# Recommender attention kernel: masked and weighted sums each in one piece, query one tile late, ordered first loads, 17 row dots on VectorE

## The chip, the cores and the metric

The kernel runs on one core of one Trainium2 chip. The metric is the device time of one execution in microseconds (us). Engines are named as in the profile: PE is TensorE, DVE is VectorE, ACT is ScalarE, POOL is GpSimd, SP is SyncE.

## The reference

For each of 512 users there are 200 history items of 128 numbers, with a mask, an age and a popularity per item. All is float32 but the mask. Cut to what matters:

```python
decay = exp(-(softplus(decay_alpha) + 1e-6) * age) * mask
mean_hist = (items * mask[..., None]).sum(1) / (mask.sum(1) + 1e-6)
q = mean_hist @ Wq.T; k = items @ Wk.T; v = items @ Wv.T
scores = (q . k) * 128**-0.5 + log(decay + 1e-12)      # -inf where masked
long_term = softmax(scores) @ v
# short_term, mean_pop, mean_rec: means over the 5 items at positions cnt-5 .. cnt-1
g = sigmoid([mean_pop, mean_rec] @ gate_w.T + gate_b)
user = g * short_term + (1 - g) * long_term
out = layernorm(user) * ln_gamma + ln_beta
```

The kernel never forms k and v. It multiplies the mean with the product of Wq and Wk once (`wqk`), takes the dot of that query with each item row, and applies Wv to the weighted sum of rows.

## The kernel before, in words

**Tiles.** A tile is 16 users, 3,200 rows of items. It lies on 128 partitions: 8 partitions to a user and 25 rows of 128 numbers on each partition, 1.6 MB in one load. There are 32 tiles, in 16 pairs; 4 pairs (8 tiles, 128 users) make a group, and there are 4 groups. `x` has 8 slots in SBUF; the load of tile n waits until the weighted sums of tile n-8 are done (L235).

**One tile's way through the engines.** POOL spreads the mask into a block matrix (`build_mblk`, L277). PE multiplies it with the 25 rows, which gives the masked sums (50 matmul records, L368). ACT divides by the count (`copy_sums`, L480), PE folds that to a mean (`make_mean`, L375), ACT copies it (L491), PE turns it into the query (`make_query`, L382) and ACT copies the query to SBUF (`copy_query`, L498). Then the 25 row dots are shared out. DVE does 18 of them as one instruction with an accumulator read each (`dots`, L734), reading the query from PSUM. For the other 7, POOL multiplies (`products`, L297, in chunks of 4 and 3 rows) and ACT sums each row (`sum_products`, L471). DVE adds the logarithm of the decay and takes the maximum over each user's 8 partitions in five small steps for a pair of tiles (`user_maxima`, L681 to L707). ACT exponentiates (L506), POOL spreads the weights (`build_pblk`, L286), PE makes the weighted sums (L368), ACT copies them (L487) and PE folds them into the group's bank (`fold_rows`, L390).

**Groups.** Once a group's eight tiles are folded, DVE, PE and POOL finish it (Wv, the short-term sum, the norm) in between the dots of the next group. For this POOL gathers the last five items of each user once a group (`gather`, L330 and L333), and raises the variance to a power (L305).

**Order.** Each engine works through an order that is written out by hand, in steps of one pair. All waits are on semaphores, and an engine that waits does nothing that stands behind. On PE a step does the masked sums of one tile, then the weighted sums of an earlier tile, cut at `CUTS` into three pieces: the mean is put between the first and the second, the query between the second and the third. So the query of a tile is made in that tile's own half step. On ACT the copy of a query stands in front of the last sums of the tile before it. Weighted sums run five tiles behind masked sums (`WX_BEHIND`).

**Start.** SP issues the mask for all tiles in one load whose runs are 25 bytes (`mask_p`), three weight loads, the mask by user, the first tile, five small loads, the second tile, the ages, the third tile, and then waits for eight gathers of POOL before the fourth tile (L249). DVE waits for all five small loads (L599) before the start of the decay's scale. POOL issues those eight gathers (L355) in a row before its first products. DVE prepares the decay and the gate between the dots of the first tiles (L613 to L651), with short vectors held in SBUF.

Of the kernel before, what the change touches and what calls it, by code (L numbers as in the profile page):

```python
# [42 lines left out]
SLOTS = GP * PAIR  # L43
# [3 lines left out]
CUTS = ((7, 15), (3, 11))  # L47
SUM_COL, WX_COL = (0, 0), (1, 1)
MEAN_AT = 2 * D
WX_BEHIND = 5  # L50
LAST_PAIR = NPAIR - 1

KEPT_AT, FIRST_KEPT = 9, 4
# [6 lines left out]
DOTS = 18  # L60
GPROD = ROWS - DOTS
GCHUNKS = ((0, 4), (4, GPROD))
POOL_IDENT = 5
POOL_IOTA = 7
POOL_CONSTANTS = 15
DVE_BANKS = 3
# [4 lines left out]
def build(nc, items, mask, age, pop, Wq, Wk, Wv, gate_w, gate_b, gamma, beta, decay_alpha, out):  # L71
    items_t = items.rearrange("u t d -> (u t d)").rearrange("(g p n) -> g p n", p=P, n=ROWS * D)
    items_rows = items.rearrange("u t d -> (u t) d")
    mask_t = mask.rearrange("u t -> (u t)").rearrange("(g p r) -> p g r", p=P, r=ROWS)
    age_t = age.rearrange("u t -> (u t)").rearrange("(g p r) -> p g r", p=P, r=ROWS)
# [4 lines left out]
    with ctx:  # L80
# [20 lines left out]
        mask_p = sb("mask_p", [P, NTILE, ROWS], U8)  # L101
        mask_f = sb("mask_f", [P, NTILE, ROWS])
        mask_u = sb("mask_u", [P, NGROUP, NITEM], U8)
        age_p = sb("age_p", [P, NTILE * ROWS])
        decay = sb("decay", [P, NTILE * ROWS])
# [3 lines left out]
        valid = sb("valid", [P, NGROUP, LAST])  # L109
        pop_valid, age_valid = sb("pop_valid", [P, NGROUP, LAST]), sb("age_valid", [P, NGROUP, LAST])  # L110
        cnt_p = sb("cnt_p", [P, NTILE])
        st = sb("st", [P, 16, NGROUP])
        soft = sb("soft", [P, 8])
# [25 lines left out]
        wx = sb("wx", [P, PAIR, D])  # L139
# [15 lines left out]
        own_v, rden_v = ps_dve[:, at + 2 * D:at + 2 * D + TU], ps_dve[:, at + 2 * D + TU:at + 2 * D + TU + 1]  # L155
        c_query = tuple(b[:, 0:D] for b in ps_query)
# [3 lines left out]
        ld_weights, ld_mask_p = sem("ld_weights"), sem("ld_mask_p")  # L160
        ld_mask_u, ld_age_p, ld_small = sem("ld_mask_u"), sem("ld_age_p"), sem("ld_small")
        last_gathered = sem("last_gathered")
        pool_setup, dve_setup, act_setup = sem("pool_setup"), sem("dve_setup"), sem("act_setup")
        wqk_done, wqk_ready = sem("wqk_done"), sem("wqk_ready")
        sp_exp_in, sp_exp, sp_ln_in, sp_ln, alpha_ready, decay_exp = (
            sem("sp_exp_in"), sem("sp_exp"), sem("sp_ln_in"), sem("sp_ln"), sem("alpha_ready"), sem("decay_exp"))
        decay_floored, decay_ln = sem("decay_floored"), sem("decay_ln")
# [29 lines left out]

        def has(s, back, n=NPAIR):

            return 0 <= s - back < n  # L200
# [19 lines left out]
        def _(sp):  # L220
# [5 lines left out]
            def load(s, k, t):  # L226
                i = k * PAIR + t
                sp.dma_start(x[:, i, :], items_t[bass.ds(s * PAIR + t, 1), :, :].rearrange("g p n -> (g p) n")
                             ).then_inc(x_loaded[i], 16)

            def step(g, k):
                s = g * GP + k
                for t in range(PAIR):
                    if has(s, GP):
                        sp.wait_ge(wx_done, (s - GP) * PAIR + t + 1)  # L235
                    load(s, k, t)

            sp.dma_start(mask_p[:, :, :], mask_t).then_inc(ld_mask_p, 16)
            for dst, src in ((wq, Wq), (wk, Wk), (wv, Wv)):
                sp.dma_start(dst[:, :], src).then_inc(ld_weights, 16)  # L240
            sp.dma_start(mask_u[:, :, :], mask_n).then_inc(ld_mask_u, 16)
            load(0, 0, 0)
            sp.dma_start(gw[:, :], gate_w.broadcast_to([P, 2])).then_inc(ld_small, 16)
            for dst, src in ((da, decay_alpha), (gb, gate_b), (gam, gamma), (bet, beta)):
                sp.dma_start(dst[:, :], src.unsqueeze(0).broadcast_to([P, src.shape[0]])).then_inc(ld_small, 16)
            load(0, 0, 1)
            sp.dma_start(age_p[:, :].rearrange("p (g r) -> p g r", r=ROWS), age_t).then_inc(ld_age_p, 16)
            load(1, 1, 0)
            sp.wait_ge(last_gathered, 2 * NGROUP * 16)  # L249
            load(1, 1, 1)  # L250
            steps(step, NPAIR - 1, first=2)
# [6 lines left out]
        def _(pool):  # L258
# [12 lines left out]
            def build_mblk(s, k):  # L271

                for t in range(PAIR):
                    if has(s, 2):
                        pool.wait_ge(sum_done, (s - 2) * PAIR + t + 1)
                    m = mask_f[:, bass.ds(s * PAIR + t, 1), :].rearrange("p g r -> p (g r)")
# [60 lines left out]
            def step(g, k):  # L337
                s = g * GP + k
                if has(s, 1):
                    products(s - 1, k - 1, 1)  # L340
# [521 lines left out]
```

## Time and profile before

| what | us |
|---|---|
| median of 3 runs | 196.67 (195.12 to 198.18) |
| the profiled execution, its own time | 197.98 |
| its span, first to last instruction | 196.2 |
| DVE busy | 162.5 |
| PE busy | 154.2 |
| POOL busy | 142.8 |
| ACT busy | 110.2 |

The profiled execution is one run. Its span leaves out 1.8 us of its own time, and that time is 1.3 us above the median. Busy times are per engine and overlap each other.

### The profile page before, as it was taken

How to read it: one execution, taken by the hardware profiler on the slowest of the kernel's cores; microseconds unless marked ns; L12 is line 12 of the kernel's file. 1: busy time of each engine (PE TensorE's matmuls, PEld its weight loads, DVE VectorE, ACT ScalarE, POOL GpSimd, SP SyncE). 2: the span in 40 equal slices, each digit the busy share in tenths (PEclk: the TensorE clock that was granted, in tenths of full speed). 3: DMA queues.
4: the chain of work that ended last, by engine and by line, in shares of the span. 5: the costliest groups of instructions: out<-in, count | busy, mean ns of one | idle time of the engine just before them, and what ended most of it. 6: DMA issues, size and time to landing. Idle time of an engine off the chain costs nothing.

```text
span 196.2 us, 9396 instructions
## 1 busy us (share of the span) xinstructions
PE 154.2 (79%) x3413; PEld 122.0 (62%) x3413; DVE 162.5 (83%) x1345; ACT 110.2 (56%) x646; POOL 142.8 (73%) x167
## 2 busy tenths in 40 slices
PE   0254734886999797999999899898997977998890
PEld 0152523573787676787787677677785756777780
DVE  1521999999999999869999998969999876958943
ACT  2002074595587566477778667655777455478420
POOL 3367984587779896777998989786989687467411
PEclk9999988698799999699999999999999999699998
DMA  6949979999589999889899899999888999400000
GB/s 35 279 171 329 189 261 398 435 429 408 185 309 331 404 356 336 314 319 336 326 384 354 345 428 354 348 358 342 323 326 303 419 352 337 160 5 17 5 3 13
DMA packets 15710, 55.57 MB, mean 283 GB/s; under 512 B 10160, under 2 KB 11312, under 8 KB 11568
## 3 DMA queue, kind: packets, MB, share of 16 engines
q1 hardware_dynamic: 15088, 53.64, 76.0%
q0 software_dynamic: 576, 1.33, 2.0%
q8 instruction: 27, 0.44, 0.9%
q14 instruction: 19, 0.16, 0.2%
HBM read 54.70 MB, written 0.26 MB: 280 GB/s over the span
## 4 chain that ended last, share of the span: by engine, by line
POOL 29%; PE 28%; issue 17%; DMA 13%; ACT 6%; DVE 5%; POOLq 0%; DVEq 0%; ACTq 0%
PE ps_acc L368 22%; POOL gprod L297 14%; DMA x<-in_r_hist_items_dram 10%; POOL mblk L277 4%; POOL pblk L286 4%; ACT gprod L471 3%; PE ps_query L382 3%; DMA mask_p<-in_r_hist_mask_dram 3%; DVE junk_v L734 3%; POOL pop_taken L355 2%; POOL age_taken L355 2%; PE ps_acc L375 2%; PE ps_group L390 2%; ACT sums L480 1%; DVE decay L617 1%
## 5 line engine op out<-in xcount | busy, mean ns | idle before, releaser
L734 DVE SCALAR_TENSOR_TENSOR junk_v<-x,ps_query 128x128 f32<-128x128 f32 x576 | 127.9, 278 | 12.7 <-ACT query L498 12.6
L297 POOL TENSOR_TENSOR gprod<-x,query 128x512 f32<-128x512 f32 x64 | 72.2, 1150 | 21.6 <-ACT query L498 21.5
L368 PE MATMUL ps_acc<-x,mblk 128*16 128x128 f32 x1600 | 66.1, 300 | 11.0 <-DMA x<-in_r_hist_items_dram 7.9
L368 PE MATMUL ps_acc<-x,pblk 128*16 128x128 f32 x1600 | 70.7, 281 | 3.3 <-issue 1.8
L471 ACT ACTIVATE gprod<-gprod 128x128 f32<-128x128 f32 x224 | 66.1, 299 | 3.8 <-POOL gprod L297 3.7
L368 PEld LDWEIGHTS ps_acc<-x,mblk 128*16 128x16 f32 x1600 | 51.9, 105 | 18.5 <-DMA x<-in_r_hist_items_dram 9.8
L368 PEld LDWEIGHTS ps_acc<-x,pblk 128*16 128x16 f32 x1600 | 45.5, 98 | 10.3 <-issue 3.4
L734 DVE DVE_READ_ACCUMULATOR junk_v<-x,ps_query 128x1 f32 x576 | 46.6, 81 | 0.1
L471 ACT ACTIVATION_READ_ACCUMULATOR gprod<-gprod 128x1 f32 x224 | 42.8, 191 | 0.0
L480 ACT ACTIVATE sums<-ps_acc,rcnt_rows 128x128 f32<-128x128 f32 x32 | 11.7, 366 | 43.5 <-PE ps_acc L368 43.5
L286 POOL TENSOR_TENSOR pblk<-own,ex 128x400 f32<-128x400 f32 x32 | 27.2, 868 | 10.9 <-ACT ex L506 10.9
L277 POOL TENSOR_TENSOR mblk<-own,mask_f 128x400 f32<-128x400 f32 x32 | 27.1, 867 | 4.7 <-DVE mask_f L581 4.6
L382 PE MATMUL ps_query<-wqk,mean_p 128*128 128x128 f32 x64 | 16.7, 345 | 4.8 <-ACT mean_p L491 4.8
L375 PE MATMUL ps_acc<-fold,sums 128*128 128x16 f32 x64 | 12.9, 276 | 8.0 <-ACT sums L480 7.8
L375 PEld LDWEIGHTS ps_acc<-fold,sums 128*128 128x128 f32 x64 | 9.8, 193 | 13.7 <-ACT sums L480 13.7
L382 PEld LDWEIGHTS ps_query<-wqk,mean_p 128*128 128x128 f32 x64 | 10.2, 200 | 11.2 <-ACT mean_p L491 10.6
L487 ACT ACTIVATE wx<-ps_acc 128x128 f32<-128x128 f32 x32 | 8.5, 270 | 5.5 <-PE ps_acc L368 3.9
L506 ACT ACTIVATE ex<-kept,nmax_p 128x25 f32<-128x25 f32 x32 | 9.7, 307 | 2.8 <-DVE nmax_p L707 2.8
L390 PEld LDWEIGHTS ps_group<-fold,wx 128*128 128x128 f32 x64 | 8.5, 189 | 3.9 <-issue 3.4
L498 ACT ACTIVATE query<-ps_query 128x128 f32<-128x128 f32 x32 | 8.6, 270 | 4.1 <-PE ps_query L382 3.0
L390 PE MATMUL ps_group<-fold,wx 128*128 128x16 f32 x64 | 10.2, 268 | 0.3 <-ACT wx L487 0.3
L491 ACT ACTIVATE mean_p<-ps_acc 128x128 f32<-128x128 f32 x32 | 8.8, 273 | 1.5 <-PE ps_acc L375 1.4
(98 smaller groups left out, 90.8 us busy)
## 6 DMA issues: line engine op xcount, KB each, us to landing
x<-in_r_hist_items_dram SPq DMA_DIRECT2D x32, 1600.0 KB, 9.2
age_p<-in_r_hist_age_hours_dram SPq DMA_DIRECT2D x1, 400.0 KB, 14.5
out_dram<-y SPq DMA_DIRECT2D x4, 64.0 KB, 4.2
mask_p<-in_r_hist_mask_dram SPq DMA_DIRECT2D x1, 100.0 KB, 6.0
mask_u<-in_r_hist_mask_dram SPq DMA_DIRECT2D x1, 100.0 KB, 3.3
wq<-in_L_rec_Wq_dram SPq DMA_DIRECT2D x1, 64.0 KB, 5.6
wk<-in_L_rec_Wk_dram SPq DMA_DIRECT2D x1, 64.0 KB, 3.6
wv<-in_L_rec_Wv_dram SPq DMA_DIRECT2D x1, 64.0 KB, 3.5
```

The costliest lines, as they stand in the source:

```text
L277: nc.gpsimd.tensor_tensor(mblk[:, k % 2, t, :, :], own[:, :].unsqueeze(1).broadcast_to([P, ROWS, TU]), m.unsqueeze(2).broadcast_to([P, ROW ...
L286: nc.gpsimd.tensor_tensor(pblk[:, k % 2, t, :, :], own[:, :].unsqueeze(1).broadcast_to([P, ROWS, TU]), ex[:, t, :].unsqueeze(2).broadcast_ ...
L297: nc.gpsimd.tensor_tensor(gprod[:, t, a * D:b * D].rearrange("p (r d) -> p r d", d=D), rows((k % GP) * PAIR + t, r0 + a, r0 + b), query[:, ...
L368: ins = nc.tensor.matmul(dst[c:c + TU, 0:D], blk[:, k % 2, t, m, :], x[:, i + t, m * D:(m + 1) * D], start=(m < CG), stop=(m >= ROWS - CG))
L375: nc.tensor.matmul(mean_cols(s, t), sums[:, t, :], fold[:, :], start=True, stop=True).then_inc(mean_done, 1)
L382: nc.tensor.matmul(c_query[t], mean_p[:, t, :, :].rearrange("p u c -> p (u c)"), wqk[:, :], start=True, stop=True).then_inc(query_done, 1)
L390: ins = nc.tensor.matmul(ps_group[:, c + t * TU:c + (t + 1) * TU], src[:, t, :], fold[:, :], start=True, stop=True)
L471: ins = nc.scalar.activation(src, src, ACT.Copy, accum_out=score[:, k % 2, t, DOTS + r:DOTS + r + 1])
L480: nc.scalar.activation(sums[:, t, :], sum_bank(s, t)[:, 0:D], ACT.Copy, scale=rcnt_rows[:, bass.ds(s * PAIR + t, 1)]).then_inc(sum_copied, 1)
L491: nc.scalar.activation(mean_p[:, t, :, :], mean_cols(s, t).unsqueeze(2).broadcast_to([P, TU, PU]), ACT.Copy).then_inc(mean_copied, 1)
L506: nc.scalar.activation(ex[:, t, :], kept[:, t, 0:ROWS], ACT.Exp, bias=nmax_p[:, t:t + 1], accum_out=wsum[:, i:i + 1]).then_inc(exp_done, 1)
L734: ins = V.scalar_tensor_tensor(out=junk_v[:, t, r, :], in0=x[:, (k % GP) * PAIR + t, r * D:(r + 1) * D], scalar=1.0, in1=c_query[t], op0=A ...
```

## The change

- **PE and ACT order.** The order is by slots of one tile. In slot n PE does the masked sums of tile n in one piece, the weighted sums of tile n-6 in one piece, the query of tile n-1, the mean of tile n, and after every second tile a fold at one place. `WX_BEHIND` is 6. Tiles 0 to 5 keep mean and query in their own slot. On ACT the copy of the query of tile n-1 stands behind all row sums of tile n-2 in the slots after the lead.
- **Buffers.** `x` has 10 slots; the weighted copy `wx` has two.
- **Row dots.** `DOTS` is 17. POOL multiplies and ACT sums 8 rows, in chunks of 4 and 4.
- **First transfers.** Mask and ages come as four blocks each of 32 partitions with long runs, and are brought to their tile layout by a transpose on DVE. Two mask blocks and the scalar `decay_alpha` are issued by ACT. SP issues tile 0 as its third load, and no longer waits for POOL's gathers. POOL issues two of the eight small gathers before its first products and the others in slots 1, 3 and 5.
- **Setup on DVE.** Most short vectors of the gate are in PSUM; the small constant is ACT's bias and not a DVE pass; the order of the pieces is changed; `wv` is turned later.

The core of the diff:

```diff
-SLOTS = GP * PAIR
+SLOTS = 10
-WX_BEHIND = 5
+WX_BEHIND = 6
-KEPT_AT, FIRST_KEPT = 9, 4
+KEPT_AT, FIRST_KEPT = 6, 4
-DOTS = 18
+DOTS = 17
@@ sync
+            def load(n):
+                i = n % SLOTS
+                if n >= SLOTS:
+                    sp.wait_ge(wx_done, n - SLOTS + 1)
+                sp.dma_start(x[:, i, :], items_t[n, :, :]).then_inc(x_loaded[i], 16)
+            for j in range(BLOCKS // 2):
+                sp.dma_start(mask_s[j * Q32:(j + 1) * Q32, :], mask_t[j, :, :]).then_inc(ld_mask_s, 16)
+            load(0)
+            for dst, src in ((wq, Wq), (wk, Wk)):
                 sp.dma_start(dst[:, :], src).then_inc(ld_weights, 16)
             sp.dma_start(mask_u[:, :, :], mask_n).then_inc(ld_mask_u, 16)
+            load(1)
+            for j in range(BLOCKS):
+                sp.dma_start(decay_s[j * Q32:(j + 1) * Q32, :], age_t[j, :, :]).then_inc(ld_age_s, 16)
+            load(2)
...
+            for n in range(4, NTILE):
+                load(n)
@@ gpsimd
+            def slot(n):
+                g, i = divmod(n, SLOTS_OF_GROUP)
+                if tile(n - WX_BEHIND + 1):
+                    build_pblk(n - WX_BEHIND + 1)
+                if i == 0 and has(g, 2, NGROUP):
+                    inverse_deviation(g - 2)
+                if tile(n + 2):
+                    build_mblk(n + 2)
+                if tile(n) and query_slot(n) == n:
+                    products(n)
+                if tile(n - 1) and query_slot(n - 1) == n:
+                    products(n - 1)
+                if i == 4 and g < NGROUP:
                     gather(g)
+                if n in (1, 3, 5):
+                    gather_context((n + 1) // 2)
@@ tensor
+            def slot(n):
+                g, i = divmod(n, SLOTS_OF_GROUP)
+                w = n - WX_BEHIND
+                if tile(n):
+                    masked_sums(n)
+                if n == 0:
+                    pe.wait_ge(ld_weights, 32)
+                    nc.tensor.matmul(ps_group[:, 0:D], wq[:, :], wk[:, :], start=True, stop=True).then_inc(wqk_done, 1)
...
+                if tile(w):
+                    weighted_sums(w)
+                if tile(n - 1) and query_slot(n - 1) == n:
+                    make_query(*divmod(n - 1, PAIR))
+                if tile(n):
+                    make_mean(*divmod(n, PAIR))
+                if tile(n) and query_slot(n) == n:
+                    make_query(*divmod(n, PAIR))
+                if tile(w - 1) and w % PAIR == 0:
+                    fold_pair(w // PAIR - 1)
@@ scalar
+            def slot(n):
+                w = n - WX_BEHIND
+                if n < WX_BEHIND:
+                    lead_slot(n)
+                else:
+                    if tile(n - 1) and query_slot(n - 1) == n:
+                        copy_mean(n - 1)
+                    if tile(n - 2) and query_slot(n - 2) == n - 1:
+                        sum_products(n - 2, 0, 2)
...
+                    if tile(n):
+                        copy_sums(n)
+                    if n > WX_BEHIND and tile(n - 2):
+                        sum_products(n - 2, 2, GPROD)
+                    if tile(n - 1) and query_slot(n - 1) == n:
+                        copy_query(n - 1)
...
+                if n % PAIR == 0 and n >= 2 * PAIR and n < NTILE + 1:
+                    exponential(n - 2 * PAIR)
+                    exponential(n - 2 * PAIR + 1)
...
+                if tile(w):
+                    copy_weighted(w)
@@ vector
+            def setup_mask():
+                dve.wait_ge(ld_mask_s, 16 * BLOCKS)
+                link(V.tensor_copy(hide_s[:, :], mask_s[:, :]))
+                V.transpose(mask_f[:, :, :].rearrange("p g r -> p r g"),
+                            hide_s[:, :].rearrange("p (q r) -> p r q", r=ROWS)).then_inc(mask_ready, 1)
...
+            setup_mask()
+            setup_counts()
+            setup_alpha()
+            setup_inverse_counts()
+            setup_hidden()
+            setup_wqk()
+            setup_first_rows()
             step(0, 0)
+            setup_valid()
+            steps(step, NPAIR + 3, first=1)
```

## Rows read from the trace of the kernel before

**Rows 1.** The page: busy time by engine, and two lines in 40 slices.
```profile
PE 154.2 (79%) x3413; PEld 122.0 (62%) x3413; DVE 162.5 (83%) x1345; ACT 110.2 (56%) x646; POOL 142.8 (73%) x167
...
DMA  6949979999589999889899899999888999400000
GB/s 35 279 171 329 189 261 398 435 429 408 185 309 331 404 356 336 314 319 336 326 384 354 345 428 354 348 358 342 323 326 303 419 352 337 160 5 17 5 3 13
```

**Rows 2.** Windows: busy us of PE, PEld, DVE, ACT, POOL; clock, DMA share, GB/s.
```profile
50.00:170.00 120.00, 108.49 (x2574) 86.81 (x2564) 110.40 (x983) 79.66 (x481) 98.44 (x106) 0.97 0.91 341
```

**Rows 3.** The page's groups of instructions: busy, mean ns of one, idle before.
```profile
L734 DVE SCALAR_TENSOR_TENSOR junk_v<-x,ps_query 128x128 f32<-128x128 f32 x576 | 127.9, 278 | 12.7 <-ACT query L498 12.6
L471 ACT ACTIVATE gprod<-gprod 128x128 f32<-128x128 f32 x224 | 66.1, 299 | 3.8 <-POOL gprod L297 3.7
```

**Rows 4.** Timeline of DVE, start and duration in us: dot, mask step, dot.
```profile
106.33 0.28 DVE L734 SCALAR_TENSOR_TENSOR junk_v<-x,ps_query 128x128 f32<-128x128 f32 x1
...
106.54 0.20 DVE L681 TENSOR_TENSOR kept<-score,ps_dve 128x50 f32<-128x50 f32 x1
106.66 0.28 DVE L734 SCALAR_TENSOR_TENSOR junk_v<-x,ps_query 128x128 f32<-128x128 f32 x1
```

**Rows 5.** Timeline of POOL from the seventh tile's products to the last tile's.
```profile
55.69 2.23 POOL L297 TENSOR_TENSOR gprod<-x,query 128x512 f32<-128x512 f32 x2
...
62.70 1.68 POOL L286 TENSOR_TENSOR pblk<-own,ex 128x400 f32<-128x400 f32 x2
64.35 2.24 POOL L297 TENSOR_TENSOR gprod<-x,query 128x512 f32<-128x512 f32 x2
...
67.54 1.02 POOL L333 DMA_INDIRECT taken<-in_r_hist_items_dram,group_row  x1 [0.82 <-POOL group_row L330]
...
178.77 2.25 POOL L297 TENSOR_TENSOR gprod<-x,query 128x512 f32<-128x512 f32 x2 [0.91 <-ACT query L498]
```

**Rows 6.** The chain that ended last, start and length: the first product chunk alone.
```profile
23.49 1.22 POOL gprod L297
```

**Rows 7.** Timeline of the start: mask, counts, first sums, scale, first dot.
```profile
6.88 0.58 DVE L581 CAST mask_f<-mask_p 128x800 f32<-128x800 uint8 x1 [4.78 <-DMA mask_p<-in_r_hist_mask_dram]
7.37 0.98 DVE L582 TENSOR_REDUCE cnt_p<-mask_p 128x32 f32<-128x800 uint8 x1
...
12.46 3.15 PE L368 MATMUL ps_acc<-x,mblk 128*16 128x128 f32 x50 [0.71 <-DVE cnt_rows L594]
...
14.59 0.95 POOL L355 DMA_INDIRECT pop_taken<-n_r_hist_popularity_dram,first_row  x1 [0.30 <-issue]
...
16.88 0.35 ACT L480 ACTIVATE sums<-ps_acc,rcnt_rows 128x128 f32<-128x128 f32 x1
...
19.39 0.29 DVE L734 SCALAR_TENSOR_TENSOR junk_v<-x,ps_query 128x128 f32<-128x128 f32 x1 [2.04 <-ACT query L498]
```

**Rows 8.** Timeline of DVE's setup: the hidden rows, and three gate steps.
```profile
23.15 2.94 DVE L613 TENSOR_SCALAR hide<-mask_f 128x800 f32<-128x800 f32 x1
...
34.41 0.16 DVE L636 TENSOR_TENSOR st<-st 128x4 f32<-128x4 f32 x1
...
49.26 1.04 DVE L648 TENSOR_TENSOR st<-st 128x4 f32<-128x4 f32 x1
```

**Rows 9.** DMA issues: size, median us from issue to landing; then the loads' spread.
```profile
mask_p<-in_r_hist_mask_dram SPq DMA_DIRECT2D x1, 100.0 KB, 6.0
mask_u<-in_r_hist_mask_dram SPq DMA_DIRECT2D x1, 100.0 KB, 3.3
...
DMA to landing us min/median/max: 6.7/9.2/21.6
```

**Rows 10.** Who waited for whom: total us, times, longest.
```profile
ACT ex L506 <- DVE nmax_p L707: 2.8, 2, 1.9
```

**Rows 11.** Timeline of the drain: PE's last weighted sums.
```profile
188.71 1.70 PE L368 MATMUL ps_acc<-x,pblk 128*16 128x128 f32 x50
```

More of the change, by code:

```diff
@@ L196, in steps, with slots, tile, query_slot @@
                 step(s // GP, s % GP)
+        def slots(slot, first=0):
+            for n in range(first, NTILE + WX_BEHIND + 3):
+                slot(n)
+        def tile(n):
+            return 0 <= n < NTILE
+        def query_slot(n):
+            return n if n < WX_BEHIND else n + 1
+        def at(s, t):
+            return (s * PAIR + t) % SLOTS
         def has(s, back, n=NPAIR):
@@ L316, in _ @@
                                 allow_small_or_imprecise_dtypes=True))
-            link(nc.gpsimd.tensor_copy(own_rows[:, :, :], own[:, :].unsqueeze(1).broadcast_to([P, CG * 2, TU])))
-            pool.wait_ge(mask_ready, 1)
-            build_mblk(0, 0)
+            assert made[0] == POOL_IOTA
             link(nc.gpsimd.memset(fold[:, :], 0.0))
@@ L357, in _ @@
                         in_offset=bass.IndirectOffsetOnAxis(ap=first_row[:, q:q + 1], axis=0)).then_inc(last_gathered, 16)
-            steps(step, NPAIR + 3)
+            pool.wait_ge(rows_ready, 1)
+            gather_context(0)
+            slots(slot)
             assert made[0] == POOL_CONSTANTS
@@ L379, in make_query @@
                 pe.wait_ge(mean_copied, s * PAIR + t + 1)
+                if not has(s, 1):
+                    pe.wait_ge(wqk_ready, 1)
                 if has(s, 1):
@@ L453, in _ @@
             pe.wait_ge(pool_setup, POOL_CONSTANTS)
-            pe.wait_ge(wqk_ready, 2)
             pe.wait_ge(cnt_ready, 1)
@@ L458, in _, with sum_products @@
             pe.wait_ge(dve_setup, DVE_BANKS)
-            steps(step, NPAIR + 3)
+            slots(slot)
         @block.scalar
         def _(act):
-            def sum_products(s, k, t, a, b):
+            def sum_products(n, a, b):
+                s, t = divmod(n, PAIR)
                 if a == 0 and has(s, 2):
@@ L551, in _ @@
             act.wait_ge(rcnt_rows_ready, 1)
-            step(0, 0)
-            act.wait_ge(alpha_ready, 1)
-            act.wait_ge(ld_age_p, 16)
-            nc.scalar.activation(decay[:, :], age_p[:, :], ACT.Exp, scale=soft[:, 5:6]).then_inc(decay_exp, 1)
-            act.wait_ge(decay_floored, 1)
-            nc.scalar.activation(decay[:, :], decay[:, :], ACT.Ln).then_inc(decay_ln, 1)
-            step(0, 1)
-            act.wait_ge(gate_in, 1)
-            nc.scalar.activation(st[:, 12:14, :], st[:, 10:12, :], ACT.Exp).then_inc(gate_exp, 1)
-            steps(step, NPAIR + 2, first=2)
+            slots(slot)
         @block.vector
```

395 lines of the change are left out of this document (184 added, 211 removed).

## The prediction, made before the changed kernel was run

> **What bounds the kernel now.** The page first: DVE is busy 83% of the span and POOL 73% [rows 1]. A share is only an average, so the windows come next. From 50 to 170 us DVE is busy 110.4 of 120 us, PE 108.5, POOL 98.4 and ACT 79.7, at a DMA share of 0.91 and 341 GB/s [rows 2]. Four resources lie within a quarter of each other. The groups name DVE's load, the 576 row dots, and what they wait for when they wait: ACT's copy of the query, 12.6 us in all, nearly all at the start [rows 3, 7].
>
> The timeline gives true prices, for DVE instructions overlap: a dot every 0.21 us (the mean of one is 278 ns), and 0.12 us for a maximum step between two dots [rows 4]. With five such steps a pair, a tile costs DVE 18 x 0.21 + 0.3 = 4.08 us. A group's finish and short-term sum are some 15 more instructions; at about 0.25 us each, between the two prices and the 0.35 us of longer ones (an estimate), that is 3.7 us a group.
>
> The steady stretch runs from the products of tile 6 at 55.69 to those of tile 31 at 178.77 [rows 5]: 123.1 us for 25 tiles, 4.92 each. DVE's sum for it is 25 x 4.08 = 102, three finishes 11.1, and about 4 for the last gate pieces: 117. So DVE alone explains all but 5%. POOL's sum before: products 2.24, two block builds 1.65 (from 62.70 to 64.35), so 3.89 a tile [rows 5]. The first 55.7 us are poor: the first dot starts at 19.39 [rows 7], and data comes at 35 to 329 GB/s in the first six slices, though 435 is reached in the eighth [rows 1].
>
> **The change part by part.**
>
> *First transfers.* Before, the mask's cast starts at 6.88 after a landing of 6.0 us [rows 7, 9]. Four blocks with long runs are issued from about 0.8 to 1.3 on two queues. The same bytes in longer runs land in 3.3 us (the mask by user) [rows 9]. I take 3.5 us, since the blocks are first in line: landed at 4.8; the other end is 6.0 us, landed at 7.3. Cast 0.58, then a transpose of 25 blocks of 32 columns, which no row shows: at the pace of the count over the same 800 elements it is 0.98 [rows 7]; the end above is the 2.94 of the slow pass over 800 elements [rows 8]. I take 1.1, nearest to the count. Mask ready at 6.6, counts at 7.7, PE's count sum and its copy to 8.4. Tile 0 is issued third, at about 1.7; the quickest load took 6.7 us [rows 9], so it also lands at 8.4. The first masked sums take 3.15 [rows 7], to 11.6. From ACT's first copy (16.88) to the first dot (19.39) it is 2.5 us [rows 7]; the weights' product now stands between, with 0.4 uncovered. First dot: 11.6 + 0.1 + 2.5 + 0.4 = 14.6, 4.8 us earlier. The decay's scale no longer waits for the other small loads. The other DVE setup ahead of the first dot (counts, scale, inverse, hidden rows, first rows) ends near 14.5 too: hidden by PE's masked sums, and if the hidden rows take 2.94 again, still inside them.
>
> On the two queues for the mask, the trace has no row. The Trainium skill (DMA: Bandwidth & Descriptors, "Issuing engines are not separate DMA queues") says that transfers issued from different engines share the same 16 DMA engines and that only issue time is saved. By that the second queue is worth about two issues, under 1 us; the sum above takes the gain from the run length and would stay.
>
> *Lead.* POOL starts when the first rows are known, about 14.7. The eight small gathers stood in one row ahead of its products at 1.25 us each (0.95 and the 0.30 before it) [rows 7]; now two do, six lie in slots 1, 3 and 5. Nothing of them is saved, they are only moved. Until the products of tile 6: two gathers 2.5, one block 0.8, then six products, ten blocks 8.3, six gathers 7.5, one group gather 2.0. Products with two chunks of four: a chunk of four is 1.22 [rows 6], so the chunk of three is about 1.0, and eight rows cost 2.49; six are 14.9. Sum 36.0: tile 6's products start at 50.7, against 55.69, 5 us earlier. DVE would be there near 45 (six tiles at 3.87, setup 7), so in the lead POOL is now last and the dot taken from DVE brings nothing there. Short vectors in PSUM help the gate: the same four-column product took 0.16 in one place and 1.04 in another, beside busy POOL [rows 8], and four such steps were slow. That is about 3 us, on DVE, which is no longer last here: costed at nothing.
>
> *Steady stretch.* DVE: 17 x 0.21 + 0.3 = 3.87 a tile; 25 tiles 96.8, finishes 11.1, rest 1: 109. POOL: 2.49 + 1.65 = 4.14 a tile, 103.5; three group gathers at 1.84 (1.02 and the 0.82 before it) [rows 5] and a small copy each, 6.1; three powers, no dearer than a block build, at most 2. POOL's sum is 111.6 and **POOL becomes the most loaded engine**. ACT: eight rows at 0.30 [rows 3] and six copies and exponentials of about 0.25, under 4 us a tile. PE loses a piece boundary and a wait on ACT's copy; since it is busy 108 of 120 with those waits in it, this gives slack and no time of its own. I keep the 5% that the stretch showed above its largest sum: 117.2 us instead of 123.1.
>
> *Loads.* Ten slots at six tiles' lag put one more load in flight, and SP is past all waits until tile 10. The rate needed is 52.4 MB over the 150 us to the last masked sums, 350 GB/s; reached were 435 in a slice [rows 1] and 341 at share 0.91 [rows 2], 375 at full share. Taken as covered by work; if the cover goes, each tile costs 1.64 MB at 341 GB/s, 4.8 us, which is where the kernel is now.
>
> Here a rule speaks against the change. The trace's best slice is 435 GB/s [rows 1]. The Trainium skill (SBUF — State Buffer, "A bandwidth-pool intuition that's wrong") gives about 358 GB/s between HBM and a core and calls HBM nearly always the end-to-end bottleneck; slices above it disagree. By it 52.4 MB take 146 us (an estimate from that page), the last tile lands near 150 us, and rival A below could hardly go under its 177; the forecast would stay.
>
> *Tail.* Before, from the last products to the end 17.4 us. Now: 2.49, four last row sums 1.2, five maximum steps without dots between 1.2, exponential 0.3, block 0.9, five hand-overs 0.8, then 7.5 as from PE's last weighted sums at 188.71 to the end at 196.2 [rows 11]: 14.4. The ends are 13.6 and the 17.4 of now.
>
> **Sum.** Span 50.7 + 117.2 + 14.4 = 182.3, from 196.2. The profiled execution's own time lies 1.8 above its span: 184.1. It stood 1.3 above the median of the runs, so against that median I say **183 us**.
>
> **The rivals.**
>
> *A. The engines mesh.* Deeper buffers take the 5% away: 50.7 + 111.6 + 14.4, 177 us. For it: part of the 5% was PE waiting for tiles that now come earlier. Against: DVE, POOL and ACT come within 3 to 12 us of each other over 25 tiles.
>
> *B. Lockstep.* The copy of a query stands behind all eight sums of the tile before, where it stood ahead of the last chunk's. So products, last four sums, copy, products form a loop of 2.49 + 1.2 + 0.3 + hand-overs, 4.2 us, just POOL's own 4.14; each gather or group finish then stops the others as well. With 12% instead of 5% over the sum: 125 us, 191 us in all. For it: four sums nearly equal. Against: POOL has two blocks to build while ACT sums.
>
> *C. Slower: the exponential blocks ACT.* In even slots ACT meets two exponentials before the next tile's copies. They need the maxima, whose last step comes 14 dots into a tile, 14 x 0.21 + 0.6 = 3.5 us, while ACT can be there 1 us into it. If DVE is the late one, ACT stands up to 2.5 us a pair with the next query behind it. It decides from 1.4 us a pair uncovered: 12.5 pairs, 17.5 us, over 200.6; all of it gives 214. Against: this wait cost only 2.8 us in two places before [rows 10], and the maxima now start three dots earlier.
>
> *D. The dot moved is no gain at all.* POOL's row costs 0.25 x 32 = 8 us while DVE's 6.7 is hidden: that is already in the sum, since POOL leads it.
>
> **How the numbers follow.** Forecast 0.48 (178 to 188), A 0.22 (172 to 178), B 0.22 (187 to 196), C 0.06, other 0.02. What a measurement can tell from no change is about 2%: 192.7 to 200.6. Faster: the forecast, A and seven tenths of B, 0.86; same: the rest of B, 0.07; slower: C and other, 0.07. The range reaches down to 173.5, which takes in the tail's and the mask's lower ends, and up to 192.5, which takes in B to its middle and the upper ends of mask and transpose (4 us).
>
> **What would show it.** First dot near 14.6 and tile 6's products near 51: start right. A steady stretch with POOL at 95% or more busy and DVE under it: forecast. Both under 90% with waits on the query's copy: B. Long waits of the exponential on the maxima: C. PE waiting long for tiles at a DMA share of 1: the loads. If the stretch per tile stays at 4.9 us, the prediction's main step is wrong.

## The result, and the profile after

| what | before | after |
|---|---|---|
| median of 20 runs each, us | 197.39 (193.71 to 201.57) | 201.62 (197.05 to 205.08) |
| ratio after to before | | 1.0147, 95% interval 1.0084 to 1.021 |
| the profiled execution, its own time | 197.98 | 204.02 |
| its span | 196.2 | 202.3 |

The changed kernel is slower by 1.5%, and certainly not faster; the forecast was 183 us and its range ended at 192.5. The profiled execution of it is one of its longer runs; five of the 20 took 197 to 200, so a few us of what follows belong to that run alone.

The page of after, busy times, the two lines in 40 slices and the queue by which PE gets its instructions (packets, MB, share of 16 engines), to be set beside [rows 1]:

```profile
PE 152.1 (75%) x3413; PEld 127.7 (63%) x3413; DVE 153.1 (76%) x1285; ACT 120.6 (60%) x710; POOL 151.9 (75%) x167
...
DMA  5999989999789899889999999998798802000000
GB/s 142 300 347 353 363 348 428 417 416 404 303 273 337 318 375 354 323 327 326 342 360 372 369 340 344 385 327 304 276 334 314 342 16 68 2 3 18 0 3 13
...
q8 instruction: 27, 0.44, 0.9%
```

No engine is above 76%. DVE has lost 9.4 us of work and POOL has gained 9.1, as the change says, and the span has grown. Two windows of after, columns as in [rows 2]: the one of [rows 2], and the steady stretch alone.

```profile
50.00:170.00 120.00, 99.53 (x2504) 86.85 (x2498) 98.65 (x882) 84.24 (x513) 102.47 (x103) 0.96 0.85 315
```

```profile
60.00:165.00 105.00, 87.67 (x2216) 76.37 (x2212) 92.12 (x830) 75.83 (x462) 90.49 (x91) 0.97 0.88 329
```

All four are idle 12% or more of the steady stretch, PE too, at 83% busy. So the answer lies in what they wait for. The groups, as in [rows 3]:

```profile
L811 DVE SCALAR_TENSOR_TENSOR junk_v<-x,ps_query 128x128 f32<-128x128 f32 x544 | 122.4, 280 | 21.2 <-ACT query L537 21.1
L314 POOL TENSOR_TENSOR gprod<-x,query 128x512 f32<-128x512 f32 x64 | 80.4, 1277 | 20.4 <-ACT query L537 20.2
L502 ACT ACTIVATE gprod<-gprod 128x128 f32<-128x128 f32 x256 | 75.8, 298 | 26.8 <-POOL gprod L314 25.3
```

DVE and POOL wait for ACT's copy of the query, and ACT waits for POOL's products: a ring. Before, the same two groups had 12.7 us (DVE) and 3.8 (ACT) of idle time [rows 3]. And of who waited for whom (total us, times, longest), one line of PE, which was 4.3 us in 7 times before:

```profile
PE ps_acc L392 <- issue: 12.9, 10, 2.4
```

The three stretches in which the prediction was summed:

| stretch | before | forecast | after | against forecast |
|---|---|---|---|---|
| start to the products of tile 6 | 55.69 | 50.7 | 56.97 | +6.3 |
| products of tile 6 to those of tile 31 | 123.1 (4.92 a tile) | 117.2 | 125.0 (5.00) | +7.8 |
| from there to the end | 17.4 | 14.4 | 20.3 | +5.9 |

**Start.** The timeline of after's start, as [rows 7]:

```profile
3.60 0.58 DVE L638 CAST hide_s<-mask_s 128x800 f32<-128x800 uint8 x1 [1.39 <-DMA mask_s<-in_r_hist_mask_dram]
4.22 1.70 DVE L639 STREAM_TRANSPOSE mask_f<-hide_s 128x800 f32<-128x800 f32 x1
...
9.74 3.14 PE L392 MATMUL ps_acc<-x,mblk 128*16 128x128 f32 x50 [2.05 <-issue]
...
15.64 0.28 DVE L811 SCALAR_TENSOR_TENSOR junk_v<-x,ps_query 128x128 f32<-128x128 f32 x1
```

The first dot is 3.75 us earlier than at 19.39 [rows 7], of 4.8 forecast. The rest is tile 0. It was issued at 1.70 and took 8.0 us to land, where 6.7 was counted, so it was there at 9.65, and PE starts at 9.74. The profile marks PE's 2.05 us of idle time "issue", but they are this wait; every run of the new order below has it, 2.05 to 2.69 us long. The DMA view of 0 to 3 us:

```profile
x<-in_r_hist_items_dram SPq DMA_DIRECT2D x1, 1600.0 KB, 8.0
```

**Lead.** The gain is gone by tile 6. ACT, POOL and DVE between 46 and 57 us:

```profile
51.96 0.32 ACT L548 ACTIVATE ex<-kept,nmax_p 128x25 f32<-128x25 f32 x1 [5.31 <-POOL pblk L302]
```

```profile
50.03 0.95 POOL L376 DMA_INDIRECT age_taken<-in_r_hist_age_hours_dram,first_row  x1 [0.30 <-issue]
...
56.97 2.51 POOL L314 TENSOR_TENSOR gprod<-x,query 128x512 f32<-128x512 f32 x2 [2.64 <-ACT query L537]
```

```profile
55.89 0.17 DVE L709 TENSOR_TENSOR pop_valid<-pop_taken,ps_fin 128x20 f32<-128x20 f32 x1 [7.59 <-DMA age_taken<-in_r_hist_age_hours_dram,first_row]
```

From the products of tile 5 (46.05) to those of tile 6 are 10.9 us, where 4.14 and two gathers (2.5) were counted. POOL does products, the last two small gathers (48.74 to 50.98) and then a block build. ACT's exponential waits 5.31 us for that build, and behind it on ACT stands the mean of tile 6; PE's next sums wait for the mean, the query comes behind them, and POOL then waits 2.64 us for the query. DVE stands 7.59 us for the last gather, to start the gate. The chain that ended last does not run through this wait, so whether it cost anything isn't shown.

**Steady.** Of the 25 spacings, 16 are 4.63 to 4.69 us; POOL shows why:

```profile
106.15 2.52 POOL L314 TENSOR_TENSOR gprod<-x,query 128x512 f32<-128x512 f32 x2 [0.48 <-ACT query L537]
108.61 0.87 POOL L302 TENSOR_TENSOR pblk<-own,ex 128x400 f32<-128x400 f32 x1
109.44 0.87 POOL L292 TENSOR_TENSOR mblk<-own,mask_f 128x400 f32<-128x400 f32 x1
110.80 2.52 POOL L314 TENSOR_TENSOR gprod<-x,query 128x512 f32<-128x512 f32 x2 [0.48 <-ACT query L537]
```

POOL's own work takes 4.17 and 0.48 is a wait each time. On ACT, from the end of those products (113.32) on:

```profile
113.35 0.31 ACT L502 ACTIVATE gprod<-gprod 128x128 f32<-128x128 f32 x1 [0.24 <-POOL gprod L314]
...
114.83 0.29 ACT L502 ACTIVATE gprod<-gprod 128x128 f32<-128x128 f32 x1
115.12 0.25 ACT L537 ACTIVATE query<-ps_query 128x128 f32<-128x128 f32 x1
```

Six sums, one each 0.295 us, and then the copy: 2.51 (products) + 1.77 + 0.25 + hand-overs 0.12 = 4.65. The call `sum_products(n - 2, 2, GPROD)` waits for the whole of the products, both chunks, before its first row; so six rows stand behind the second chunk and not the chunk's own four.

The other nine spacings are longer, 4.74 to 6.40: three have a group's gather (6.19 to 6.28), and four of the other six follow times in which **PE stands still with nothing to wait for** (the 6.40 follows the 2.42 us below). PE in the stretch between two of them, and the matmul behind the second (columns of windows; then the timeline, its idle time in brackets):

```profile
82.59:88.71 6.12, 5.90 (x126) 0.72 0.80 289
88.71:94.93 6.22, 4.67 (x126) 1.00 0.95 341
94.93:115.73 20.80, 19.50 (x505) 1.00 0.95 363
115.73:121.93 6.20, 5.39 (x126) 1.00 0.94 343
...
142.98:153.87 10.89, 9.26 (x252) 1.00 0.85 314
```

```profile
143.00 1.16 PE L392 MATMUL ps_acc<-x,mblk 128*16 128x128 f32 x33 [2.42 <-issue]
```

Between two pauses lie 126, 252 or 505 matmuls, multiples of 126 to within one, and each has its weight load: 252 instructions. The program has 3413 + 3413 of them, and 27 packets on the instruction queue: 253 to a packet. So PE pauses when it comes to the end of a block of instructions and the next is not there.

The trace also has the times of these packets; narrow windows of the DMA view place them. The window of 140.5 to 141.5 us holds the one that belongs to the pause above, from 140.58 to 141.47:

```profile
q8 instruction: 1, 0.02, 5.5%
```

Each of after's nine pauses in its sums (the wait for tile 0 is not one of them) ends 1.3 to 1.5 us after such a packet. In the fifteen traces of this document, 97 of the 99 pauses after 60 us end 1.2 to 1.7 us after one. Late is the packet's start and not its length: counted from PE's first matmul of the block before, the packet starts after 3.7 us in the median in after and 3.3 in before, but after 0.7 and 0.5 in e11 and e12 below, whose loads are light; it takes about 1 us in all four. Whether PE asks late or the request waits is not shown.

**Tail.** PE waits 2.92 us for the block of weights, which now stands behind the products of tile 31 on POOL, and then 100 matmuls take 5.29 us, 3.23 before. The window gives a granted clock of 0.60 of the upper level of 2.4 GHz, so most of it ran at 1.2:

```profile
185.34 2.46 PE L392 MATMUL ps_acc<-x,pblk 128*16 128x128 f32 x50 [2.92 <-POOL pblk L302]
188.70 5.29 PE L392 MATMUL ps_acc<-x,pblk 128*16 128x128 f32 x100
```

```profile
188.60:194.00 5.40, 5.40 (x102) 0.60 0.00 0
```

### The profile page after: what moved, and what is told of

It is laid out like the page before. It is cut to its first block, busy times and chain, and to the rows that moved or that the text cites. A ratio compares the mean times of both kernels' runs of the same rounds, so it can differ in the third digit from the quotient of the medians.

```text
span 202.3 us, 9424 instructions
## 1 busy us (share of the span) xinstructions
PE 152.1 (75%) x3413; PEld 127.7 (63%) x3413; DVE 153.1 (76%) x1285; ACT 120.6 (60%) x710; POOL 151.9 (75%) x167
## 4 chain that ended last, share of the span: by engine, by line
POOL 44%; issue 25%; DMA 12%; PE 8%; SPq 5%; ACT 4%; POOLq 1%; DVE 0%; ACTq 0%
POOL gprod L314 22%; DMA x<-in_r_hist_items_dram 12%; POOL pblk L302 10%; POOL mblk L292 8%; PE ps_acc L392 7%; ACT gprod L502 2%; POOL taken L352 2%; SPq L259 1%; SPq L249 1%; PE ps_query L408 1%; POOL rstd L322 1%; ACT ex L548 1%; SPq L265 1%; ACT query L537 1%; POOL pop_taken L376 0%
## 5 line engine op out<-in xcount | busy, mean ns | idle before, releaser
L811 DVE SCALAR_TENSOR_TENSOR junk_v<-x,ps_query 128x128 f32<-128x128 f32 x544 | 122.4, 280 | 21.2 <-ACT query L537 21.1
L314 POOL TENSOR_TENSOR gprod<-x,query 128x512 f32<-128x512 f32 x64 | 80.4, 1277 | 20.4 <-ACT query L537 20.2
L502 ACT ACTIVATE gprod<-gprod 128x128 f32<-128x128 f32 x256 | 75.8, 298 | 26.8 <-POOL gprod L314 25.3
L392 PE MATMUL ps_acc<-x,pblk 128*16 128x128 f32 x1600 | 60.6, 291 | 18.8 <-ACT mean_p L528 10.0
L392 PE MATMUL ps_acc<-x,mblk 128*16 128x128 f32 x1600 | 64.8, 303 | 11.4 <-issue 7.8
L392 PEld LDWEIGHTS ps_acc<-x,pblk 128*16 128x16 f32 x1600 | 49.8, 102 | 25.5 <-issue 16.4
L392 PEld LDWEIGHTS ps_acc<-x,mblk 128*16 128x16 f32 x1600 | 50.0, 106 | 18.0 <-issue 9.6
L502 ACT ACTIVATION_READ_ACCUMULATOR gprod<-gprod 128x1 f32 x256 | 48.3, 189 | 0.0
L811 DVE DVE_READ_ACCUMULATOR junk_v<-x,ps_query 128x1 f32 x544 | 44.9, 83 | 0.0
L513 ACT ACTIVATE sums<-ps_acc,rcnt_rows 128x128 f32<-128x128 f32 x32 | 11.4, 355 | 14.9 <-PE ps_acc L392 14.8
L408 PE MATMUL ps_query<-wqk,mean_p 128*128 128x128 f32 x64 | 17.1, 352 | 2.7 <-ACT mean_p L528 2.6
L376 POOL DMA_INDIRECT pop_taken<-n_r_hist_popularity_dram,first_row x4 | 4.1, 1037 | 8.7 <-DVE first_row L665 8.3
L322 POOL TENSOR_TENSOR rstd<-vare,half 128x1 f32<-128x1 f32 x4 | 2.3, 569 | 10.0 <-DVE vare L849 10.0
```

The costliest lines, as they stand in the source:

```text
L314: nc.gpsimd.tensor_tensor(gprod[:, t, a * D:b * D].rearrange("p (r d) -> p r d", d=D), rows(at(s, t), r0 + a, r0 + b), query[:, s % 2, t, ...
L392: ins = nc.tensor.matmul(dst[c:c + TU, 0:D], blk[:, s % 2, t, m, :], x[:, at(s, t), m * D:(m + 1) * D], start=(m < CG), stop=(m >= ROWS - CG))
L408: nc.tensor.matmul(c_query[t], mean_p[:, t, :, :].rearrange("p u c -> p (u c)"), wqk[:, :], start=True, stop=True).then_inc(query_done, 1)
L502: ins = nc.scalar.activation(src, src, ACT.Copy, accum_out=score[:, s % 2, t, DOTS + r:DOTS + r + 1])
L513: nc.scalar.activation(sums[:, t, :], sum_bank(s, t)[:, 0:D], ACT.Copy, scale=rcnt_rows[:, bass.ds(s * PAIR + t, 1)]).then_inc(sum_copied, 1)
L811: ins = V.scalar_tensor_tensor(out=junk_v[:, t, r, :], in0=x[:, at(s, t), r * D:(r + 1) * D], scalar=1.0, in1=c_query[t], op0=ALU.mult, op ...
```

## Experiments

Every run was made beside runs of the kernel before on the same chip ("before beside it"). For each profiled execution the table gives the start of tile 6's products, the mean per tile from there to tile 31, and PE's pauses of the line "issue" inside its sums, total and number, without the wait for tile 0. For after and before: 5.00 with 10.9 (9), and 4.92 with 4.3 (7).

| run | median us | before beside it | ratio, 95% | tile 6 | per tile | pauses |
|---|---|---|---|---|---|---|
| e1_split_sums | 199.43 | 199.04 | none | 58.55 | 4.97 | 12.8 (10) |
| e2_18_dots_new_order | 196.13 | 199.04 | 0.9834 (0.9767 to 0.9902) | 56.28 | 4.84 | 13.4 (11) |
| e3_17_dots_old_order | 199.56 | 199.04 | 0.9999 (0.9911 to 1.0087) | 55.30 | 5.04 | 3.1 (3) |
| e5_8_slots | 228.64 | 199.04 | none | 57.22 | 6.05 | 0.5 (1) |
| e6_two_in_flight | 196.08 | 199.31 | none | 56.86 | 4.87 | 12.4 (13) |
| e7_gathers_early | 194.58 | 199.31 | none | 53.31 | 4.78 | 15.6 (14) |
| e8_old_no_gather_wait | 202.40 | 199.31 | 1.0196 (1.0046 to 1.0346) | 57.87 | 5.00 | 7.7 (5) |
| e10_18_dots_split | 197.89 | 199.31 | 0.9912 (0.9724 to 1.0100) | 56.25 | 4.82 | 11.4 (11) |
| e11_new_light_loads | 197.67 | 198.76 | none | 58.18 | 4.84 | 1.0 (4) |
| e12_old_light_loads | 188.87 | 198.76 | 0.9534 (0.9385 to 0.9684) | 55.81 | 4.48 | 0 |
| e13_loads_in_pieces | 193.67 | 198.76 | none | 52.61 | 4.82 | 17.1 (15) |
| f2_18_early_light | 183.58 | 198.51 | 0.9428 (0.9261 to 0.9594) | 52.13 | 4.47 | 1.4 (2) |
| f1_18_early_again | 193.12 | 198.51 | 0.9878 (0.9692 to 1.0065) | 53.82 | 4.83 | 13.8 (10) |

Where the ratio is "none", only medians stand side by side.

### The ring on ACT: e1_split_sums

```diff
-                        sum_products(n - 2, 2, GPROD)
+                        sum_products(n - 2, 2, GCHUNKS[0][1])
+                        sum_products(n - 2, GCHUNKS[0][1], GPROD)
```

> The changed kernel, with the last six row sums of ACT split in two waits: rows 2 and 3 wait for POOL's first chunk alone, rows 4 to 7 for the second. Nothing else differs. Loop theory (the query's copy stands behind six sums that all wait for POOL's second chunk, which sets 4.65 us between two tiles' products): the spacing falls by the two sums, 0.59 us, to about 4.17 (POOL's own sum 4.16), and the time by 22 x 0.48 = 10 us less what other waits take back: 191 to 195 us. Rival, pauses and loads (PE's pauses and late tiles set the pace): spacing stays at 4.6 or more, time within 2 us of the changed kernel's 201.6.

POOL of e1, the products of two tiles in a row, now without a wait for the query:

```profile
105.25 2.51 POOL L314 TENSOR_TENSOR gprod<-x,query 128x512 f32<-128x512 f32 x2
...
109.54 2.53 POOL L314 TENSOR_TENSOR gprod<-x,query 128x512 f32<-128x512 f32 x2
```

The usual spacing fell from 4.65 to 4.30 (4.17 was expected), so the ring is real and was rightly named. The time did not follow: 199.43 us, where 191 to 195 was expected. The mean per tile moved only from 5.00 to 4.97, and PE's pauses rose from 10.9 to 12.8 us. So in the full run the ring is not the only thing that holds the pace.

### The moved dot: e2_18_dots_new_order and e3_17_dots_old_order

e2 is after with `DOTS = 18`; e3 is before with

```diff
-KEPT_AT, FIRST_KEPT = 9, 4
+KEPT_AT, FIRST_KEPT = 8, 4
-DOTS = 18
+DOTS = 17
```

> The changed kernel with 18 row dots on DVE and 7 on POOL and ACT (chunks 4 and 3). Loop theory: the loop is shorter by one product of POOL (0.27) and one sum of ACT (0.29): 4.65 becomes 4.09, and DVE's own 4.08 a tile plus the groups' finish becomes the largest sum, so 25 tiles take 5 to 9 us less than in the changed kernel: 193 to 197 us. Rival, 17 dots are the gain and other parts the loss: DVE, now at 4.5 us a tile with the finish, makes it 3 to 6 us slower than 201.6.

> The kernel before with 17 row dots on DVE and 8 on POOL and ACT, the maxima one dot earlier so that the last step still fits; the old order stays. If DVE bounded the kernel before as the prediction says, its 6.7 us less show at least in part: 191 to 195 us. If POOL's extra 0.27 us and ACT's 0.29 us a tile lie in the loop in the old order too, no gain or a loss: 196 to 202 us.

POOL of e2:

```profile
99.69 2.25 POOL L314 TENSOR_TENSOR gprod<-x,query 128x512 f32<-128x512 f32 x2
...
103.78 2.25 POOL L314 TENSOR_TENSOR gprod<-x,query 128x512 f32<-128x512 f32 x2 [0.20 <-ACT query L537]
```

With the dot back on DVE the new order is 5.5 us under after's 201.62 and 1.7% faster than before, with an interval clear of 1. The usual spacing is 4.09: the ring is shorter by 0.26 (products) and 0.3 (one sum). In the old order the same dot costs and gains nothing that can be measured. A likely reason is that there the copy of the query stands in front of the last sums; no run tried this alone. So the two parts of the change do not fit each other. And taking 6.7 us of dots from DVE gained nothing in the old order either, so DVE's work alone was not what held that kernel back in the full run.

### Both: e10_18_dots_split

> The changed kernel with 18 dots and ACT's last sums in two waits (rows 2 and 3 for the first chunk, rows 4 to 6 for the second). The loop of 4.09 us loses its two sums and falls to POOL's own 3.9; DVE's own sum (4.08 a tile and 3.7 a group) and the pauses of PE then set the pace. Loop theory: least spacing 3.9, gain over 18 dots alone at most 2 us, 194 to 196. Rival (DVE is the bound and its maxima are in the way): no gain, 196 to 198.

e2 and e1 together. The usual spacing is 4.02 (3.9 was expected) and the mean 4.82, both hardly under e2's 4.09 and 4.84; the median, 197.89, is above e2's. At 18 dots the ring is POOL's own length and splitting has little left to give.

### The gathers of slot 5: e7_gathers_early

```diff
-                if n in (1, 3, 5):
-                    gather_context((n + 1) // 2)
+                if n in (1, 2, 3):
+                    gather_context(n)
```

> The changed kernel with 18 dots, the small gathers in slots 1, 2 and 3 in place of 1, 3 and 5. Lead theory (the 10 us between the products of tiles 5 and 6 come from the gathers of slot 5: DVE waits for the last of them, ACT's exponential for POOL's block behind them): products of tile 6 start at 51 to 54 us and not at 56.3, and the time falls by 2 to 5 us, to 191 to 194. Rival (PE at its lower clock sets the lead): products of tile 6 stay within 1 us of 56.3, time as with 18 dots alone, 196.

On top of e2. Tile 6's products start at 53.31 instead of 56.28, 3.0 us earlier, and the profiled span is 3.2 us less than e2's. f1_18_early_again is the same kernel with more runs:

> The changed kernel with 18 dots and gathers in slots 1, 2, 3 once more, in five rounds, for an interval against the kernel before: if the row of dots given to POOL and the gather of slot 5 were the losses, it stands at 0.965 to 0.985 of before; if the 194.6 of its first run was luck, at 0.99 to 1.00.

It has the lowest median of the kernels that compute the whole, 193.12 against 198.51 beside it, but its interval just takes in 1, and 0.9878 is just above the 0.965 to 0.985 expected.

### What PE's pauses hang on

**Buffers.** e5 is after with `SLOTS = 8`.

> The changed kernel with 8 slots for tiles in place of 10, so that at most one or two loads stand in the queue while PE works. Theory on PE's pauses (12 us of pauses inside runs of matmuls, all before the last load lands, come from queued loads ahead of the instruction fetch): fewer loads in flight give shorter pauses, under 8 us, but late tiles come instead. Rival (the pauses have nothing to do with the depth of the load queue): pauses as before at 10 to 13 us, and late tiles make it slower by 3 to 10 us.

```profile
PE ps_acc L392 <- DMA x<-in_r_hist_items_dram: 38.6, 19, 3.8
...
PE ps_acc L392 <- issue: 3.0, 2, 2.6
```

The ten slots are needed: at six tiles' lag eight make PE wait 38.6 us for tiles. Of the 3.0 us marked "issue", 2.59 are the wait for tile 0, so one pause of 0.45 is left. Two things changed at once: PE is slower, so its instructions have more time to come, and the DMA share from 60 to 165 us is 0.75 and not 0.88. The run does not tell them apart.

**Depth of the load queue.** e6 is e2 with SP waiting for tile n-2 before it issues tile n; **size of its pieces**: e13 is e7 with each tile in five loads of five rows.

> The changed kernel with 18 dots (196.1 us, 18 us of PE pauses), and SP issues tile n, from 4 on, only when tile n-2 has landed: at most two loads in flight, ten slots as before. Queue theory (PE's pauses inside runs of matmuls come from its instruction fetch standing behind queued loads): the pauses fall from 18 us to under 8, the tiles still come in time, 25 tiles take 5 to 8 us less, 189 to 192 us. Rival (the pauses come from PE using up its instructions in bursts, whatever is queued): pauses stay at 14 to 20 us, time within 2 us of 196, or above if tiles come late.

> The changed kernel with 18 dots and gathers in slots 1, 2, 3 (194.6 us), and each tile loaded by five transfers of 5 rows (2,560 bytes a partition) and not by one of 25 rows (12,800 bytes). If a fetch of instructions waits for the transfer that an engine is in, shorter ones let it in sooner: pauses fall from 18.7 us to under 9, time 188 to 192 us. Rival (the fetch waits for its share of full engines, whatever the piece): pauses 14 us or more, time 193 to 197.

Neither lowers the pauses much: 12.4 us (13) with at most two tiles in flight, for 13.4 (11) in e2, and 17.1 (15) with pieces of 2,560 bytes for 12,800, for 15.6 (14) in e7. Smaller pieces do not help. On the depth e6 says less than it seems to: e2's loads land after 10.2 us in the median, one is issued every 4.84 us, and so about two were in flight there anyway (8.3 us in e6). It shows that the deeper queue of the first 50 us is not the cause; fewer than two in flight was not tried.

**The pace of the loads.** From the first reuse of a slot on, only 8 of 25 rows are loaded, in after and in before:

```diff
-                sp.dma_start(x[:, i, :], items_t[n, :, :]).then_inc(x_loaded[i], 16)
+                c = (ROWS if n < SLOTS else 8) * D
+                sp.dma_start(x[:, i, 0:c], items_t[n, :, 0:c]).then_inc(x_loaded[i], 16)
```

> The changed kernel, but from tile 10 on only 8 of the 25 rows of each tile are loaded (the other rows are stale data of an earlier tile); all other work is the same. Fetch theory (PE's pauses stand at every 252nd matmul and weight-load record, where it fetches its next block of instructions, and last as long as that fetch waits for DMA engines that are full of tile loads): after about 50 us no pause over 0.3 us, the sum of pauses falls from 14.5 to under 5 us, spacing 4.65 almost everywhere, 25 tiles in 121 to 123 us, time 195 to 198. Rival (the pauses are PE's own, whatever the DMA does): pauses stay above 10 us and the time within 2 us of 201.6.

> The kernel before, from tile 8 on only 8 of 25 rows loaded (the rest stale). It has 4 us of pauses and 8 us of waits for tiles; both go. If these are what keeps it above DVE's sum, 25 tiles take 117 to 119 us and not 123.1, time 189 to 193 us. Then the old order without its DMA losses is faster than the new order without its own. Rival (the old order's own waits set it): less than 3 us gained.

The steady window of e11, of e12 and, for comparison, of before:

```profile
60.00:165.00 105.00, 92.93 (x2362) 80.43 (x2356) 94.41 (x851) 78.72 (x482) 94.28 (x95) 1.00 0.39 114
```

```profile
60.00:165.00 105.00, 99.42 (x2474) 81.67 (x2467) 103.83 (x949) 76.33 (x462) 93.46 (x101) 1.00 0.41 124
```

```profile
60.00:165.00 105.00, 94.13 (x2256) 75.28 (x2250) 96.68 (x879) 69.71 (x422) 88.41 (x96) 0.98 0.93 349
```

At a DMA share of 0.4 neither kernel has a pause above 0.2 us in this window. In before it is worth a lot: 10 us, DVE at 99% of the window, 4.48 a tile. That is 112.0 us for the 25 tiles, where 117 to 119 was expected: waits for tiles went too (7.9 to 0.5 us), and DVE's own sum is smaller than it was priced. In after only a little: 22 of its 25 spacings are 4.63 to 4.69 and the three others are the gathers at 6.2. There the ring is the bound, and nothing hides it: 120.9 us for 25 tiles. With loads out of the way the kernel before is 8.8 us faster than the changed one (188.87, 197.67); in full runs it is 4.2.

The single spacings are the same with and without load, 4.65 in after and e11; it is not a general slowing down of the engines. The Trainium skill (SBUF — State Buffer, "A bandwidth-pool intuition that's wrong") says as much: contention there is structural and not a shared total. The trace agrees for POOL's and ACT's work; the instruction fetch it does not speak of.

### How far the order could go: f2_18_early_light

> The changed kernel with 18 dots and gathers in slots 1, 2, 3, from tile 10 on only 8 of 25 rows of a tile loaded (the rest stale). If the loads (through PE's pauses and late tiles) are what keeps this version at 4.78 us a tile where its loop is 4.09, then 25 tiles take 107 to 110 us and the time is 184 to 188. Rival (DVE's own sum, 4.08 a tile and the groups' finish, or the gathers): 25 tiles still take 115 us or more, time 191 or more.

e7 with the light loads. Its steady window:

```profile
60.00:165.00 105.00, 93.25 (x2456) 83.31 (x2454) 104.44 (x956) 76.72 (x469) 94.09 (x100) 1.00 0.37 110
```

DVE is busy 104.44 of 105 us, and the new order reaches 183.58: 5.3 us under the old one with light loads. Its steady stretch is no shorter, though: 111.7 us for 25 tiles, 112.0 in e12. What the traces show of the gain is ahead of it, the products of tile 6 at 52.13 and not at 55.81. With full loads the same kernel (f1) takes 193.12. So 9.5 us of it are taken by the loads.

### SP's wait in the old order: e8_old_no_gather_wait

```diff
-            sp.wait_ge(last_gathered, 2 * NGROUP * 16)
```

> The kernel before with one line out: SP no longer waits for the small gathers ahead of the fourth tile. If the late fourth tile (masked sums at 35 us) cost the kernel before anything, products of tile 6 start 2 to 4 us earlier than 55.7 and the time falls by as much, to 193 to 196 us. If the lead is set by POOL's gathers and DVE's setup, nothing changes: within 1 us of before.

```profile
22.54 0.61 PE L374 MATMUL ps_acc<-fold,sums 128*128 128x16 f32 x2 [7.23 <-issue]
```

Taking the wait out of the old order costs 2%, where a gain or nothing was expected: the early loads run at a share of 1.02 from 20 to 30 us, and PE stands 7.23 us for nothing that the trace shows. (Part of such a pause is in other runs of the old order too: 4.33 us ahead of 19.57 in e3, 6.12 ahead of 21.01 in e12. So its size here is not the wait's alone.) It is not one of the pauses above: it comes after 55 matmuls, and the first packet of that queue starts at 28.26. Its cause is open.

## Why the prediction was wrong

- **Mask and first dot: nearly right.** Cast at 3.60 where 4.8 was said; the transpose took 1.70, between the bounds of 0.98 and 2.94 but above the 1.1 taken. The first dot came at 15.64, for 14.6. The mask was ready at 5.92, before the 6.6 said; what came late was tile 0, landed at 9.65 and not at 8.4.
- **Lead: wrong by 6.3.** The sum took POOL as last and its work as packed: 36.0 us from 14.7. POOL starts at 16.02, 1.3 us later, and waits 4.7 us for queries in three places, 2.64 of it ahead of tile 6, where the gathers of slot 5 hold back the block that ACT waits for. "Nothing of them is saved, they are only moved" priced the gathers on their own engine and not for what stands behind them. e7, with the gathers earlier, gives back 3.0 us.
- **Steady stretch, the step that failed most: +7.8.** "POOL's sum is 111.6" plus 5% was the step. With light loads the same kernel still takes 120.9 us (e11), 3.7 over the 117.2; the other 4.1 come with full loads. The 3.7 are the ring: the loop of rival B was priced with four sums behind the products: "2.49 + 1.2 + 0.3 + hand-overs, 4.2 us, just POOL's own 4.14". It has six, 4.65, since one call waits for both chunks (e1: 4.30 when it doesn't). Over 25 tiles the 0.51 above 4.14 is 12.8 us. Against it stand the 5.6 us that the sum's 5% added, and the gathers and powers, which cost 4.6 us (three spacings of 6.2) and not 8.1. With seven rows on POOL the spacing is 4.09 and the kernel faster than before (e2). Rival B was the right mechanism; "products, last four sums, copy" was the term mis-sized, and its chance of 0.22 rested on the two being equal. Its 191 us was too low as well.
- **PE "gives slack".** It was read from busy time. PE stood still 10.9 us in nine pauses, in which it waits for nothing that the prediction looked for; the 4.3 us of before were in its trace and were not read. They are longer in the faster runs, 13.4 us in e2 and 15.6 in e7, and 0.5 in the slow e5. The 5% that the sum kept from before was partly this, and it isn't a percentage of work.
- **"DVE alone explains all but 5%": wrong.** DVE's sum of 117 us was too high. With light loads the same work takes 112.0 us in e12 and 111.7 in f2, with DVE at 99%. So 11.1 of the 123.1 us, and not 6, were waits that came with full loads, and a dot taken from DVE gained nothing there (e3).
- **Loads "taken as covered".** They came in time: PE waited for tiles 3.6 us in after, 7.9 before. But they cost by another way as well, the instruction fetch. All that the loads cost together is 10 us in the old order (e12) and 9.5 in the best new one (f1, f2); PE's pauses went from 4.3 to 0 us and from 13.8 to 1.4. The rule that the prediction set against the change, 358 GB/s at most between HBM and a core, is not what bound it: slices of after show 428 and 417 GB/s, 20.8 us in a row 363, and its steady mean, 329, is under that figure.
- **Tail: +5.9.** The sum was too short before anything went wrong. From the products of tile 31 to PE's last weighted sums it counted 6.9 us; e2, with the same order and the upper clock there, takes 9.6 and has a tail of 17.1, and after takes 12.7. In after PE waits 2.92 us for the block (1.25 at that place in before), and the granted clock of 0.60 for the last 100 matmuls costs 2.1, the difference to the 3.23 us of before. Both are read from the trace; no run tried them, and part belongs to that execution: the tails of e11 and e1, with the same number of dots, are 18.6 and 18.7 us.
- **Rivals A and C.** The engines meshed only in f2, where the loads were light: 111.7 us, and A's 111.6 is met by chance, since there DVE leads and not POOL. The wait of the exponential on the maxima (C) was 1.2 us in all, less than the 2.8 of [rows 10].
- The test that the prediction set, "if the stretch per tile stays at 4.9 us, the prediction's main step is wrong", came out: 5.00.

**Still open.** Why PE's next block of instructions starts late under full loads isn't known; a deep queue and the size of the pieces are not it. Nor were the new start and the one-piece order put each by itself into the old kernel, and the tail's two parts weren't tried.

## What to carry to other kernels

When a copy is moved behind a call that waits, count what that call waits for and every instruction behind it, and write the ring out to its last row: 0.3 us a row over 25 tiles is 7.5 us, more than the 5.9 forecast for the steady stretch. Idle time of PE marked "issue" is to be read before PE is called slack. First look whether a load landed just then, as with tile 0 here. Then count the instructions between two such pauses and look when the packets of the instruction queue end: if they fit, a faster order can pay part of its gain back there. A kernel in which several engines lie within 10% of each other is best compared once with its loads made light: that shows what a change is worth without them (8.8 us against it here, 4.2 in full runs), and what each engine's own sum is.

## What the runs showed of the hardware

- PE stops 0.2 to 3.1 us at multiples of 252 instructions while the DMA engines are busy 0.80 to 0.95 of the time, 3 to 17 us in a run, and hardly at a share of 0.4. 97 of 99 such stops end 1.2 to 1.7 us after a packet of 16 KB on the instruction queue. With full loads that packet starts 3.7 us (after) and 3.3 us (before) after the block before is begun, in the median, with light ones 0.5 to 0.9 (e12, e11, f2), and itself takes about 1 us.
- At most two loads in flight for about two, and runs of 2,560 for 12,800 bytes, make no clear difference to it (12.4 for 13.4 us, 17.1 for 15.6).
- A transpose on DVE of 128x800 float32 in blocks of 32 took 1.70 us, three times the cast of as many elements from bytes (0.58).
